# Work of a quantising phase moved into the attention before it, and its output bias moved from GpSimd to TensorE

## What is computed

```python
x = x + tanh(g_xattn[l]) * xattn_l(layernorm(x), ctx)
x = x + tanh(g_ffn[l]) * ffn_l(layernorm(x))          # l = 0 .. 3
```

```python
def quant_act_uint8(x):                    # one scale for the whole tensor
    s = max(max(x), EPS) / 255.0
    return clip(round(x / s), 0, 255) * s, s
def quant_weight_int8_perchannel(w):       # one scale for each row
    s = max(max(abs(w), axis=1), EPS) / 127.0
    return clip(round(w / s), -128, 127) * s, s
def quant_bias_int32(b, s_in, s_w):
    return round(b / (s_in * s_w)) * (s_in * s_w)
def quant_linear(x, w, b):
    return einsum(xq, wq) + bq
h = relu(quant_linear(x, w1, b1))          # w1: 1024 x 256
y = quant_linear(h, w2, b2)                # w2: 256 x 1024
```

## Time and profile before

| what | value |
|---|---|
| median of 3 runs | 1591.49 us (1585.51 to 1594.08) |
| profiled execution, its own time | 1586.5 us |
| its span | 1584.7 us, mean granted TensorE clock 0.899 |
| busy: TensorE, VectorE, ScalarE, GpSimd | 84%, 45%, 30%, 19% |
| chain that ended last: TensorE, VectorE, GpSimd, issue, ScalarE | 75%, 13%, 4%, 3%, 3% |
| the two slices from 554 to 634 us: TensorE busy | 3 and 5 tenths |

### The profile page before, as it was taken

One profiled execution on the slowest core, in us unless ns is written; L12 is line 12 of the kernel. 1 busy time (PEld: TensorE's weight loads), 2 busy tenths in 40 slices (PEclk: granted clock), 3 DMA queues, 4 the chain that ended last, 5 costly groups with the idle time before them and its releaser, 6 DMA issues.

```text
span 1584.7 us, 17797 instructions
## 1 busy us (share of the span) xinstructions
PE 1333.0 (84%) x6201; PEld 783.8 (49%) x6201; DVE 713.1 (45%) x2010; ACT 478.0 (30%) x890; POOL 303.0 (19%) x373
## 2 busy tenths in 40 slices
PE   5999979779998935799887699985778867999997
PEld 2545443334755622464444476753333434666664
DVE  5755253574334289775554322226334445211214
ACT  1244434302122127024342133321543311222220
POOL 5100010041000013330212222232512222122220
PEclk9799989979999968779998699996888787899999
DMA  9990010010000010300003622221000020445425
GB/s 241 257 295 12 1 50 0 0 57 1 0 1 0 1 30 1 120 1 1 25 21 115 182 65 62 63 101 63 1 0 28 28 82 28 149 133 159 151 80 168
DMA packets 93798, 109.90 MB, mean 69 GB/s; under 512 B 10546, under 2 KB 86063, under 8 KB 93583
## 3 DMA queue, kind: packets, MB, share of 16 engines
q1 hardware_dynamic: 86718, 89.87, 19.7%
q0 software_dynamic: 6992, 18.88, 3.3%
HBM read 59.87 MB, written 48.86 MB: 69 GB/s over the span
## 4 chain that ended last, share of the span: by engine, by line
PE 75%; DVE 13%; POOL 4%; issue 3%; ACT 3%; DMA 1%; SPq 1%; DVEq 0%; POOLq 0%; ACTq 0%
PE bank L1097 9%; PE bank L698 5%; PE bank L1131 4%; PE bank L764 4%; PE bank L1179 4%; PE bank L1146 4%; PE bank L784 4%; PE bank L681 4%; PE bank L813 3%; PE bank L955 3%; PE bank L802 3%; PE bank L816 2%; PE bank L639 2%; PE bank L865 2%; PE bank L825 2%
## 5 line engine op out<-in xcount | busy, mean ns | idle before, releaser
L1250 ACT ACTIVATE scratch<-bank 128x512 f32<-128x512 f32 x240 | 126.1, 603 | 108.1 <-PE bank L791 49.9
L1097 PE MATMUL bank<-scratch 128*128 128x320 f32 (+3 forms) x480 | 155.1, 481 | 0.6 <-issue 0.6
L1899 DVE TENSOR_REDUCE scratch<-bank 128x2 f32<-128x308 f32 x256 | 105.8, 472 | 76.0 <-PE bank L764 71.8
L1569 POOL TENSOR_SCALAR rstd<-mv 128x4 f32<-128x4 f32 x36 | 11.0, 306 | 672.3 <-DVE mv L1684 659.0
L1097 PEld LDWEIGHTS bank<-scratch 128*128 128x128 f32 (+1 forms) x480 | 87.8, 186 | 62.3 <-issue 31.4
L1219 ACT ACTIVATE scratch<-bank 128x512 f32<-128x512 f32 x56 | 32.1, 596 | 268.1 <-PE bank L639 257.5
L2396 DVE TENSOR_TENSOR scratch<-scratch,bank 128x320 f32<-128x320 f32 (+3 forms) x60 | 31.4, 526 | 175.9 <-PE bank L1097 169.3
L639 PE MATMUL bank<-ident,scratch 128*128 128x128 f32 x224 | 44.1, 362 | 74.3 <-DVE scratch L1690 74.3
L1598 POOL DMA_INDIRECT x_slots<-scratch x64 | 65.7, 1026 | 138.1 <-DVEq L2257 120.2
L784 PE MATMUL bank<-scratch 32*128 32x512 f32 x384 | 83.8, 669 | 0.0
L764 PE MATMUL bank<-scratch 32*128 32x308 f32 x512 | 82.6, 526 | 1.3 <-DVEq L1763 1.3
(11 more groups left out here) (374 smaller groups left out, 2348.8 us busy)
## 6 DMA issues: line engine op xcount, KB each, us to landing
x_slots<-zeros SPq DMA_DIRECT2D x1, 17680.0 KB, 79.6
scratch<-in_L_ffn_W SPq DMA_DIRECT2D x16, 512.0 KB, 8.9
scratch<-y_back SPq DMA_DIRECT2D x16, 512.0 KB, 7.5
scratch<-in_L_ffn_w_gate SPq DMA_DIRECT2D x16, 352.0 KB
scratch<-in_L_ffn_w_up SPq DMA_DIRECT2D x16, 352.0 KB
x_slots<-zeros SPq DMA_DIRECT2D x1, 5200.0 KB, 97.6
scratch<-x_slots SPq DMA_DIRECT2D x39, 130.0 KB, 2.1
y_back<-zeros SPq DMA_DIRECT2D x1, 4352.0 KB, 39.4
```

Of the source, the lines that this page charges most:

```text
L1097: last = pe.matmul(bk[0:fn, 0:n], w[s][:, k, m * P:m * P + fn], moving(k), start=k == 0, stop=k == DK - 1)
L1250: act.activation(v["PT"][:, n % 2, j, :], bk[:], ACT.Exp, scale=float(v["hd"]) ** -0.5).then_inc(RP.read, 1)
L1899: dve.tensor_reduce(v["mx"][:, TPC * c + t, r, 2 * m:2 * m + 2], bk[:, 0:2 * M].rearrange("p (e k) -> p e k", k=M), AX.X, ALU.max)\
```

## The change

- ATT gets the steps `next normal c` (after front 3, back 2, back 3, tail 3) and `next weights` (after tail 2, before back 3), which work for phase 3.
- VectorE makes phase 3's statistics of chunk c at the end of tail c; GpSimd runs phase 3's `norm` at the end of its attention program; `next normal` normalises and takes the chunk's largest value.
- `round_weights` starts in back 1 and gets four more steps, the weights' conversion in halves (back 2), and the diagonals. `next weights` holds the transposes, copies and the spreading of the scales.
- In `quantised` the scale and bias of the hidden layer are made after the first chunk's rounding, the rows of the output after the first chunk's conversion, with two products fewer.
- The output bias is no longer added to X by GpSimd. TensorE adds it in each bank with a product of one row, `ones[0:1]` by `rowB[0:1]`, and waits once for `rows_made`, inside the first bank.
- wi1 moves into memory that the attention has done with, and wi2, w1T, w2T, diag, sw2r and m behind the attention's memory.

```diff
@@ ATT
-               ("front", 3), ("tail", 1), ("back", 2), ("tail", 2), ("back", 3), ("tail", 3)]
+               ("front", 3), ("next normal", 0), ("tail", 1), ("back", 2), ("next normal", 1), ("tail", 2), ("next weights", 0),
+               ("back", 3), ("next normal", 2), ("tail", 3), ("next normal", 3)]
@@ TensorE, attention
-                    else:
+                    elif what == "next weights":
+                        turned_weights(p + 1)
+                    elif what == "tail":
@@ TensorE, quantised, second product
-                                last = pe.matmul(bk[:, i * D:(i + 1) * D], v["hi"][:, f, t * P:(t + 1) * P], v["w2T"][:, f, :],
-                                                 start=f == 0, stop=f == FT1 - 1)
+                                pe.matmul(bk[:, i * D:(i + 1) * D], v["hi"][:, f, t * P:(t + 1) * P], v["w2T"][:, f, :],
+                                          start=f == 0, stop=False)
+                            if (c, q, i) == (0, 0, 0):
+                                pe.wait_ge(rows_made, 1)
+                            last = pe.matmul(bk[:, i * D:(i + 1) * D], ones[0:1, :], v["rowB"][0:1], start=False, stop=True)
@@ GpSimd
                 add_row(v["gbo"][:], gbo_made, L, p)
+                norm(p + 1)
...
                 if L == 1:
-                    norm(p)
                     for n in range(2):
                         pool.wait_ge(xmax_made, n + 1)
                         pool.partition_all_reduce(v["sc"][:, n:n + 1], v["m"][:, 60 + n:61 + n], P, RMAX).then_inc(xall_made, 1)
-                    add_row(v["rowB"][:], rows_made, 1, p)
@@ VectorE, attention
-                                if c >= 2:
+                                if c >= 1:
                                     next(rounding, None)
+                    elif what == "next weights":
+                        for _ in rounding:
+                            pass
+                        bk = RB.get(dve, p + 1, "sw2r")
+                        dve.tensor_copy(ph[p + 1]["sw2r"][:], bk[:, 0:D]).then_inc(RB.read, 1)
+                    elif what == "next normal":
+                        normalise(p + 1, c)
+                        dve.wait_ge(ln_y, lnorm(p + 1, c))
+                        u = ph[p + 1]
+                        st.did(dve.tensor_reduce(u["m"][:, c:c + 1], u["Y"][:, TPC * c:TPC * (c + 1), :], AX.XY, ALU.max))
                     else:
...
                             add_out(bk, 2 * c + q, tg[:, L:L + 1]).then_inc(RB.read, 1)
+                        dve.wait_ge(RB.read, RB.emptied)
+                        statistics(p + 1, c)
@@ VectorE, round_weights (was in quantised, whole, after x_norm(p))
+                for w, wi, n in (("w1", "wi1", FT1), ("w2", "wi2", DK)):
+                    for i in range(2):
+                        a = slice(i * n // 2, (i + 1) * n // 2)
+                        st.did(dve.tensor_scalar(v[wi][:, a], v[w][:, a], ROUND, None, ALU.subtract))
+                        yield
@@ VectorE, quantised
-                x_norm(p)
...
-                for c in range(NC):
-                    dve.wait_ge(ln_y, lnorm(p, c))
-                    st.did(dve.tensor_reduce(v["m"][:, c:c + 1], v["Y"][:, TPC * c:TPC * (c + 1), :], AX.XY, ALU.max))
...
+                    if c == 0:
+                        dve.wait_ge(RB.read, RB.n(p, "sw2r"))
+                        st.did(dve.tensor_scalar(v["rowS"][:], v["sw2r"][:], v["sc"][:, 5:6], None, ALU.mult))
+                        st.wait()
+                        st.did(dve.reciprocal(v["rowI"][:], v["rowS"][:]))
+                        st.wait()
+                        st.did(dve.tensor_tensor(v["rowB"][:], v["b2"][:], v["rowI"][:], ALU.mult))
+                        st.did(dve.tensor_scalar(v["rowT"][:], v["rowS"][:], tg[:, 5:6], None, ALU.mult))
+                        st.wait()
+
+                        st.did(dve.tensor_scalar(v["rowB"][:], v["rowB"][:], ROUND, ROUND, ALU.add, ALU.subtract))
+                        st.wait()
+                        dve.sem_inc(rows_made, 1)
-                dve.wait_ge(xbias, XB[p])
```

More of the change, by code:

```diff
@@ L245, in build @@
         ex_made = sem("exponentials_made")
[L246 removed]
+        XB = {2: 1, 4: 2, 6: 3}
         x_out = sem("x_final")
@@ L448, in build @@
                 v["rnd"] = scratch.take((1,))
+                assert scratch.at <= end16
+                scratch.at = NT * D
+                v["wi1"] = scratch.take((FT1, D), BF16)
+                assert scratch.at <= NT * D + DK * CH
+                scratch.at = end16
+                v["wi2"] = scratch.take((DK, F1), BF16)
+                v["w1T"] = scratch.take((DK, F1), BF16)
+                v["w2T"] = scratch.take((FT1, D), BF16)
+                v["diag"] = scratch.take((DK, P))
+                v["sw2r"] = scratch.take((D,))
+                v["m"] = scratch.take((64,))
             if L >= 2:
@@ L1011, in quantised @@
                 last.then_inc(RB.filled, 1)
+            def quantised(p):
+                v = ph[p]
                 for n in range(NC + 1):
@@ L1311, in attention @@
                         continue
+                    if what == "next weights":
+                        turned_weights(p + 1)
+                    if what not in ("front", "tail"):
+                        continue
                     for m in range(MT):
@@ L2077, in quantised @@
                 for d in range(DK):
-                    last = st.did(dve.tensor_scalar(v["diag"][:, d, :], ident[:], v["sw2"][:, d:d + 1], None, ALU.mult))
+                    st.did(dve.tensor_scalar(v["diag"][:, d, :], ident[:], v["sw2"][:, d:d + 1], None, ALU.mult))
                 st.wait()
                 dve.sem_inc(diag_made, 1)
-                bk = RB.get(dve, p, "sw2r")
-                dve.tensor_copy(v["sw2r"][:], bk[:, 0:D]).then_inc(RB.read, 1)
+            def quantised(p):
+                v = ph[p]
                 def scale(n):
@@ L2099, in quantised @@
                 scale(0)
-                st.did(dve.memset(v["rnd"][:], ROUND))
-                st.did(dve.tensor_scalar(v["sb1"][:], v["sw1"][:], v["sc"][:, 4:5], None, ALU.mult))
-                st.wait()
-                st.did(dve.reciprocal(v["ib1"][:], v["sb1"][:]))
-                st.wait()
-                st.did(dve.tensor_tensor(v["bq1"][:], v["b1"][:], v["ib1"][:], ALU.mult))
-                st.wait()
-                st.did(dve.tensor_scalar(v["bq1"][:], v["bq1"][:], ROUND, ROUND, ALU.add, ALU.subtract))
-                st.wait()
-                dve.tensor_tensor(v["bq1"][:], v["bq1"][:], v["sb1"][:], ALU.mult).then_inc(hscale_made, 1)
                 for c in range(NC):
@@ L2117, in quantised @@
                     dve.tensor_scalar(v["xi"][:, TPC * c:TPC * (c + 1), :], a, ROUND, None, ALU.subtract).then_inc(xi_made, 1)
+                    if c == 0:
+                        st.did(dve.memset(v["rnd"][:], ROUND))
+                        st.did(dve.tensor_scalar(v["sb1"][:], v["sw1"][:], v["sc"][:, 4:5], None, ALU.mult))
+                        st.wait()
+                        st.did(dve.reciprocal(v["ib1"][:], v["sb1"][:]))
+                        st.wait()
+                        st.did(dve.tensor_tensor(v["bq1"][:], v["b1"][:], v["ib1"][:], ALU.mult))
+                        st.wait()
+                        st.did(dve.tensor_scalar(v["bq1"][:], v["bq1"][:], ROUND, ROUND, ALU.add, ALU.subtract))
+                        st.wait()
+                        dve.tensor_tensor(v["bq1"][:], v["bq1"][:], v["sb1"][:], ALU.mult).then_inc(hscale_made, 1)
                 for c in range(NC):
@@ L2126, in quantised @@
                 dve.sem_inc(hs_ready, 1)
-                dve.wait_ge(RB.read, RB.n(p, "sw2r"))
-                st.did(dve.tensor_scalar(v["rowS"][:], v["sw2r"][:], v["sc"][:, 5:6], None, ALU.mult))
-                st.wait()
-                st.did(dve.reciprocal(v["rowI"][:], v["rowS"][:]))
-                st.wait()
-                st.did(dve.tensor_tensor(v["rowB"][:], v["b2"][:], v["rowI"][:], ALU.mult))
-                st.wait()
-                st.did(dve.tensor_scalar(v["rowB"][:], v["rowB"][:], ROUND, ROUND, ALU.add, ALU.subtract))
-                st.wait()
-                st.did(dve.tensor_tensor(v["rowB"][:], v["rowB"][:], v["rowS"][:], ALU.mult))
-                st.wait()
-                st.did(dve.tensor_scalar(v["rowB"][:], v["rowB"][:], tg[:, 5:6], None, ALU.mult))
-                st.did(dve.tensor_scalar(v["rowT"][:], v["rowS"][:], tg[:, 5:6], None, ALU.mult))
-                st.wait()
-                dve.sem_inc(rows_made, 1)
                 for c in range(NC):
```

23 lines of the change are left out of this document (9 added, 14 removed).

## The result

The changed kernel takes 1606.86 us (median, 1603.06 to 1615.88) against 1592.64 for the kernel before in the same series (1585.51 to 1595.83): ratio 1.0099, 95% interval 1.0076 to 1.0122. It is slower by 1%, where the forecast was 1572. The profiled execution took 1606.65 us, its span is 1604.9, its mean granted clock 0.884 (0.899 before).

A forecast was written before the change was run, and what follows sets the result against it. Bound around the change: VectorE, GpSimd, VectorE again; inside the attention TensorE. Attention +3.4, phase 3's start -14.4, second product -8.4, next phase +2.3 sum to -17.1 us: 1569.4 profiled, 1572 forecast, range 1562 to 1583.

The forecast's parts named there:

- two products of one row by 256 columns: Second product: adding the bias on TensorE costs 0.45 us more a bank, within a forecast gain of 8.4 us.
- 3.6 for a bank there and 2.2 for one at full clock: Second product: us per bank with its bias, 3.6 at TensorE's low clock and 2.2 at full clock; five charged at 2.2.
- there each statistic is on the path in full: 3.8 together: Attention, after tails 0 and 1: VectorE's statistics delay the negated maxima TensorE waits for, costing 3.8 us.
- TensorE's clock falls in the attention: Rival, chance 0.08: stalls lower the clock; one back's scores cost 10.7 us (1583), three backs' 32 us (1604).
- a granted clock under 1.00 between 434 and 555: Sign that the forecast is wrong: TensorE's clock below full within the attention, between those times in us.
- The start of the phase: Phase 3's start: statistics made early gain 14.4 us, after 4.3 lost to GpSimd's code change, priced at 7.5.
- The rounding moved to back 1 and the weights' turning: Attention: rounding leaving back 2 gains 5.2 us, costs 1.0 in back 1; turning the weights before back 3 costs 3.8.
- The conversions at 2.3 us: Second product: without GpSimd's adds, VectorE's three other conversions of X take 2.3 us each instead of 4.43.
- Phase 4: Next phase's start: GpSimd's change back to its old code now falls there and costs 2.3 us, bounds 0 and 5.4.
- code change hidden: Rival, chance 0.12: GpSimd's code change costs little when early or runs beside the chain; gain 23.7 us, 1565.
- worse placed: Rival, chance 0.12: GpSimd's code change stands behind the wait for phase 3's begin; gain only 11.2 us, 1578.
- the adds were not what slowed the conversions: Rival, chance 0.06: second product's conversions stay at 4.4 us without GpSimd's adds; gain only 10.7 us, 1578.

The follow-up runs named there:

- The run with the switch in its middle: Changed kernel with the f32 bias product in one row for chunks 0 and 1, in 128 rows for chunks 2 and 3: 1598.64 us, ratio 1.0049.
- the run with late statistics: Changed kernel with the statistics of chunks 0 and 1 moved behind the negated maxima of backs 1 and 2: 1594.21 us, ratio 1.0013.
- both faulty steps mended: Changed kernel with statistics of chunks 0 and 1 behind the negated maxima and the bias as one bf16 product in 128 rows: 1566.97 us, ratio 0.9865.

## Why the prediction was wrong

The two steps that failed both left out TensorE's clock.

**"two products of one row by 256 columns"**, priced at "0.45 more" a bank (second product, -8.4 forecast, +18.1 measured, 26.5 off) was the step that turned the sign. Without the bias product the stretch takes 25.8 us, and the sum without its eight times 0.45 = 3.6 us gives 25.1, so the rest of the sum, the conversions and the reads, was right. The product itself was mis-sized three times over: 29.4 us in place of 3.6. Its record was counted as half a product; in 128 rows it takes 31.8 - 25.8 = 6.0 us. Its bounds, 0.11 to 0.5 us, were taken from products in 128 rows; with 64 rows and a return each time the stretch takes 36.6 us, 4.8 more. And in one row it held the clock at 0.50 through all 46 us: another 55.2 - 36.6 = 18.6 us. (That the one-row product at full clock would cost what 64 rows cost is taken from their equal 1.15 us at the low clock.) "3.6 for a bank there and 2.2 for one at full clock" supposed that the clock would rise because TensorE was busy. The earlier trace rows had shown it at 0.55 with TensorE busy for 16.5 of 17.5 us, on products in 32 rows; it was read as a danger for the attention and not for the second product.

The Trainium skill (TensorE: Matmul & The Clock Gate, Part 1: The HAM clock gate) has the clock follow how busy TensorE has been. The run with the switch in its middle speaks against busy time as the records show it: TensorE is busy before and after 643.9, and the clock is 0.50 before and rises behind it. What the array does while busy counts too: with 64 rows in place of one, and equal busy times at the low clock, it rose.

**"there each statistic is on the path in full: 3.8 together"** was right by itself (3.7), but the forecast +3.4 for the attention came out as +11.8. The rival "TensorE's clock falls in the attention" is what happened, with 7.6 us in place of its 10.7 or 32, and it had been given 0.08; its sign, a granted clock under 1.00 between 434 and 555, came. The other 0.9 us are the weights' part, +0.5 in place of -0.4. Evidence against the rival was that the clock stayed up over waits of 0.9 us; the prediction had no row for a wait between 0.9 and 4.0, and 2.72 was enough, in back 1 and in back 2. Backs 1 and 2 also keep fewer rows of the array busy there: their masked products are of 64 and 32 rows.

**What held.** The start of the phase: 16.0 us gained, 14.4 forecast; the code change cost 5.98 us, not 7.48. The rounding moved to back 1 and the weights' turning: +0.5 us net in the run with late statistics, -0.4 forecast (-5.2 + 1.0 + 3.8); the three terms were not measured apart. The conversions at 2.3 us. Phase 4: +2.9, forecast +2.3, though the change of code took 7.97 us. The rivals "code change hidden", "worse placed" and "the adds were not what slowed the conversions" are out by these rows. With both faulty steps mended, the same change gives a ratio of 0.9865, some 21 us of 1590. The prediction's sum without the statistics' 3.8 is 20.9. Part of that closeness is chance, since the bias product is another one and the scatter behind is as large; but the mechanisms carry the gain, and the form of sixteen small products and the place of eight small instructions decide whether it is seen.

What stays open: how few rows, for how much of the time, hold the clock down. One row in f32 does, one row in bf16 and 64 rows in f32 don't; these runs don't say what the chip measures. Open too is why short falls stand behind waits of 0.67 and 0.89 us in some kernels and not in others.

## What to carry to other kernels

A small product costs more than its columns: fill the rows of the array (a constant from the identity or a block matrix does it, here at 0.85 us in place of 1.15 at the low clock), because a turn to few rows and back cost 0.2 to 0.3 us at full clock, and one-row f32 products kept the whole stretch at half clock. Before an instruction is put ahead of something that TensorE waits for, put it behind, if nothing needs it sooner: 1.8 us of added wait cost the attention 4.4 and 6.9 us, the rest of it through the clock. And a forecast for a stretch with TensorE as its bound needs two sums, one at each clock level, with a row that shows which applies to products of that shape.

## What the runs showed of the hardware that had not been expected

- A stretch with TensorE busy throughout stayed at a granted clock of 0.50 for 46 us, with 1.15 of every 2.97 us in one-row f32 products; with 128 rows in their place it rose 4 to 5 us later.
- Going from 128 rows to 64 and back costs 0.3 us a time at full clock: 0.62 and 0.98 us in place of 0.43 and 0.87. At the low clock one row and 64 rows take the same, 1.15 us, and 128 rows take 0.85.
- The clock fell to 0.50 for 6 and 13 us behind waits of 2.72 us; for about 3 us it also fell behind waits of 0.67 and 0.89 us, which elsewhere had no fall behind them.
- An f32 product is two records; counting records halves its price.
- GpSimd's change of code took 5.70 to 6.17 us into the all-reduce (the changed kernel and its versions), and 6.88 to 8.33 us back. It is paid when the first instruction that needs the other code comes up, whether or not that is ready to run: the row stands at 573.9, and the reduction that the all-reduce needs ended at 576.7. The COPY at 669.28 ran without a change.
- From one profiled execution to another, the 910 to 926 us behind the change differ by 16 us with the same instructions; in the longest TensorE's records themselves are busy 12.4 us longer.
